# Attention weights spread over a head's dimensions through DRAM instead of through TensorE

## The reference, cut to what matters

```
q, k, v = split(layernorm(x) @ W_qkv.T + b_qkv)         # 16 heads of 8 dimensions
gains = softmax(q @ W_qscale.T + scale_gain)            # 11 scales for each head and position
for j in range(11):                                     # distance 2**j
    for tau in range(4):                                # offsets 0, d, 2d, 3d
        qk = sum(q * shift(k, d*tau), over a head's 8 dimensions)
        out += gains[j] * D4[tau] * qk * shift(v, d*tau)
out += softplus(bypass) * sum(q * k) * v
x += (out * sigmoid(gate)) @ W_out.T + b_out
```

## Time and profile before

| | |
|---|---|
| median of 3 runs | 1466.12 us (1459.56 to 1484.78) |
| the profiled execution | 1464.85 us, span 1463.1 us |
| TensorE busy | 1162.0 us (79%) |
| VectorE busy | 791.5 us (54%) |
| ScalarE busy | 651.2 us (45%) |
| GpSimd busy | 791.0 us (54%) |
| DMA queue of SyncE | 88.01 MB, 21.1% of 16 engines |

### The profile page before, as it was taken

The page is one execution under the profiler, slowest core; times in us unless marked ns, Lnnn a source line. Parts: engine busy times, 40 slices in busy tenths (PEclk is TensorE's granted clock), DMA queues, the critical chain, the costliest instruction groups (busy, mean ns, idle before and its releaser), DMA issues.

```text
span 1463.1 us, 32843 instructions
## 1 busy us (share of the span) xinstructions
PE 1162.0 (79%) x9942; PEld 876.2 (60%) x9942; DVE 791.5 (54%) x1723; ACT 651.2 (45%) x2050; POOL 791.0 (54%) x1274
## 2 busy tenths in 40 slices
PE   3878887887978898889987899866998767994481
PEld 2545554565655665666565667765877655884471
DVE  4878898889866776567787567431213201240111
ACT  2233332555445654566544444553553323562241
POOL 2655457655687648754468845875125433323604
PEclk9998987999979997799999578988985567997786
DMA  4700001222221112111123112333322323443442
GB/s 125 208 1 0 1 1 51 67 62 61 80 63 55 56 37 75 43 54 40 45 66 87 43 54 61 99 99 89 99 89 72 93 68 114 118 131 109 124 132 69
DMA packets 117639, 107.59 MB, mean 74 GB/s; under 512 B 15540, under 2 KB 88541, under 8 KB 117469
## 3 DMA queue, kind: packets, MB, share of 16 engines
q1 hardware_dynamic: 106704, 88.01, 21.1%
q0 software_dynamic: 8192, 16.79, 3.9%
q10 hardware_dynamic: 2573, 0.69, 0.2%
HBM read 76.73 MB, written 28.70 MB: 72 GB/s over the span
## 4 chain that ended last, share of the span: by engine, by line
PE 39%; POOL 18%; DVE 13%; issue 10%; another core or an unknown queue 8%; ACT 7%; ACTq 1%; DMA 1%; SPq 1%; DVEq 1%; POOLq 0%
PE bank L1160 9%; PE bank L1147 8%; POOL acc L799 8%; PE bank L1187 5%; POOL mom L764 3%; POOL sorted_x L822 3%; DVE made L1312 2%; DVE term L1341 2%; PE bank L1083 2%; PE bank L1124 2%; PE bank L1051 2%; PE bank L1030 2%; PE bank L1110 2%; PE bank L1140 1%
## 5 line engine op out<-in xcount | busy, mean ns | idle before, releaser
L799 POOL TENSOR_TENSOR acc<-acc,term 128x512 f32<-128x512 f32 x219 | 281.6, 1286 | 71.3 <-DVE term L1341 53.8
L1160 PE MATMUL bank<-w,hT 128*128 x1088 | 214.9, 321 | 22.7 <-ACT hT L985 12.8
L1341 DVE TENSOR_TENSOR term<-bank,V 128x512 f32<-128x512 f32 x251 | 167.9, 684 | 71.3 <-PE bank L1110 43.6
L1005 ACT ACTIVATE hid<-bank 128x16 f32<-128x16 f32 x512 | 93.0, 182 | 253.6 <-PE bank L1187 200.9
L985 ACT ACTIVATE hT<-bank,b1T 128x128 f32<-128x128 f32 x544 | 165.4, 371 | 81.3 <-PE bank L1147 64.8
L1187 PEld LDWEIGHTS bank<-hid,abcT 128*32 128x32 f32 x4096 | 88.3, 116 | 188.1 <-ACT hid L1005 105.5
L839 POOL DMA_INDIRECT back<-sorted_y,slot_i x128 | 125.2, 978 | 138.1 <-DMA sorted_y<-ysb 52.9
L1160 PEld LDWEIGHTS bank<-w,hT 128*128 128x128 f32 x1088 | 172.3, 219 | 40.5 <-issue 35.2
L1187 PE MATMUL bank<-hid,abcT 128*32 128x16 f32 x4096 | 138.0, 200 | 65.5 <-ACT hid L1005 57.8
L1312 DVE SCALAR_TENSOR_TENSOR made<-bank,qkvb,K 128x512 f32<-128x512 f32 x251 | 176.2, 741 | 15.7 <-PE bank L1083 6.8
L1147 PE MATMUL bank<-xTb,w1b 128*128 128x128 f32 x864 | 165.6, 320 | 7.8 <-ACT xTb L973 7.6
(11 more groups left out here) (177 smaller groups left out, 2190.6 us busy)
## 6 DMA issues: line engine op xcount, KB each, us to landing
w1b<-in_W SPq DMA_DIRECT2D x130, 256.0 KB
K<-in_W SPq DMA_DIRECT2D x54, 256.0 KB, 2.7
xsb<-sorted_x SPq DMA_DIRECT2D x184, 64.0 KB
sorted_y<-ysb SPq DMA_DIRECT2D x136, 64.0 KB
X<-in_x SPq DMA_DIRECT2D x64, 64.0 KB
out_x<-X SPq DMA_DIRECT2D x64, 64.0 KB
sorted_x<-K SPq DMA_DIRECT2D x14, 256.0 KB, 3.6
sorted_y<-made SPq DMA_DIRECT2D x48, 64.0 KB
```

The source lines that it names most:

```text
L799: nc.gpsimd.tensor_tensor(acc[:], acc[:] if k > 1 else term[0][:], term[k % NTERM][:], ALU.add).then_inc(S["terms_added"], 1)
L1005: nc.scalar.activation(hid[n % 2][:, cs], bank[6 + n % 2][:, cs], ACT.Tanh).then_inc(S["h_ready"], 1)
L1160: last = nc.tensor.matmul(bank[SLOT_BANK[place(n)]][:, 0:D], tile(hT[place(n)], c), w2[:, ds(second[n] + c * D, D)], start=(c == 0), stop= ...
L1341: V_.tensor_tensor(term[k % NTERM][:], bank[2 + k % 2][:], V[:, at:at + CW], ALU.mult).then_inc(S["terms_ready"], 1)
```

## The change

`pack` stays. Its result `wt[g]` is written to DRAM (`wstore`, at most 256 KB; two buffers for each g), and for each shift one DMA reads 16 rows back, each eight times (`fetch`, 128 rows of 2 KB, 256 KB), into a ring of seven tiles `spread` in SBUF. `high`, `low` and the spreading products on TensorE go; the product for term 0 stays and moves into bank 1. A term is now made in place in its tile, from two SBUF operands; term 0 goes straight into `acc`. Both new DMAs stand in SyncE's queue, in the planner's order, with the experts' loads and stores. A fetch waits until its tile's former term has been added, seven fetches before. reduce of the next chunk waits for this chunk's packs only; qproj of the next chunk waits for term 0; the normalised chunk `xn` gets memory of its own and no longer waits for adds.

```diff
-NPROD, NTERM = 7, 4
+NPROD, SPREAD_RING = 7, 7
...
-                free = [("low", before, 2 * g + h) for h in range(len(halves(before, g)))] if i and g < 2 else [] if g < 2 else \
-                    [("spread", before, last_term(before, 2)) if i and active(before)[2] else None]
+                free = [("wstore", before, g) if i and (g < 2 or active(before)[2]) else None]
...
             piece("PE", "reduce", i, b, [0, 0.85, 1.0, 1.15, 1.35][len(x)], USUAL,
                   [("product", i, x[-1]), ("reduce", i, b - 1) if b else None,
-                   ("term", before, last_term(before)) if i else None])
+                   past("pack", before, 0), past("pack", before, 1)])
...
+        for g in range(3 if g2 else 2):
+            piece("SP", "wstore", i, g, 0.1, USUAL,
+                  [("pack2", i, 0) if g == 2 else ("pack", i, g), ("term", i - 2, last_term(i - 2)) if i >= 2 else None], lands=2.6)
         for j, s in enumerate(sums):
...
+                piece("SP", "fetch", i, j, 0.1, USUAL,
+                      [("wstore", i, s.g), ("fetch", *fetched_for(f - 1)) if f else None,
+                       ("add", *fetched_for(f - SPREAD_RING)) if f >= SPREAD_RING else None], lands=3.2)
+            piece("DVE", "term", i, j, 0.72, USUAL,
+                  [("fetch", i, j) if j else ("spread", i, 0), ("vcopy", i, 0), ("term", i, j - 1) if j else past("out", before)])
...
+                elif what == "wstore":
+                    if k < 2:
+                        sp.wait_ge(S["packed"], nth("pack", n, k))
+                    else:
+                        sp.wait_ge(S["bank0_taken"], in_turn("reduce2", n))
+                    if n >= 2:
+                        sp.wait_ge(S["terms_ready"], nth("term", n - 2, last_term(n - 2)))
+                    h = H * len(active(n)[k]) if k < 2 else H
+                    sp.dma_start(wd[k][n % 2][0:h, :], wt[k][0:h, :]).then_inc(weights_out[k][n % 2], 16)
+                elif what == "fetch":
+                    s, f = terms(n)[k], fetch_of(n, k)
+                    sp.wait_ge(weights_out[s.g][n % 2], weights_stored(n, s.g))
+                    if f >= SPREAD_RING:
+                        sp.wait_ge(S["terms_added"], nth("add", *fetched_for(f - SPREAD_RING)))
+                    sp.dma_start(spread[f % SPREAD_RING][:],
+                                 bass.AP(wd[s.g][n % 2].tensor, s.m * H * CW, [[CW, H], [0, HD], [1, CW]])).then_inc(
+                                     spread_in[f % SPREAD_RING], 16)
...
-                    nc.gpsimd.tensor_tensor(acc[:], acc[:] if k > 1 else term[0][:], term[k % NTERM][:],
+                    nc.gpsimd.tensor_tensor(acc[:], acc[:], spread[fetch_of(n, k) % SPREAD_RING][:],
                                             ALU.add).then_inc(S["terms_added"], 1)
...
-                elif what == "high":
...
-                        pe.wait_ge(S["products_ready"], nth("product", n - 1, len(products(n - 1)) - 1))
+                        pe.wait_ge(S["terms_ready"], nth("term", n - 1, 0))
...
+                    nc.tensor.matmul(bank[1][:], blkw[:], prod[j % NPROD], start=True, stop=True).then_inc(S["spread_ready"], 1)
...
-                elif what == "low":
...
+                        if n:
+                            dve.wait_ge(S["bank0_filled"], in_turn("out", n - 1))
+                        dst, weights = acc[:], bank[1][:]
+                    else:
+                        u, turn = fetch_of(n, k) % SPREAD_RING, fetch_of(n, k) // SPREAD_RING
+                        dve.wait_ge(spread_in[u], 16 * (turn + 1))
+                        dst = weights = spread[u][:]
+                    V_.tensor_tensor(dst, weights, V[:, at:at + CW], ALU.mult).then_inc(S["terms_ready"], 1)
```

More of the change, by code:

```diff
@@ L217, in timeline @@
         piece("ACT", "vcopy", i, 0, 0.7, USUAL, [("vproj", i, 0)], bank0=0)
-        piece("PE", "qproj", i, 0, 1.1, USUAL, [("xcopy", i, 0), ("product", before, nb - 1) if i else None])
+        piece("PE", "qproj", i, 0, 1.1, USUAL, [("xcopy", i, 0), past("term", before, 0)])
         for h in range(2):
@@ L268, in timeline @@
[L268 to L274, removed]
+            if j == 0:
+                piece("PE", "spread", i, 0, 1.1, USUAL, [("product", i, n - 1)])
+            else:
+                f = fetch_of(i, j)
+                piece("SP", "fetch", i, j, 0.1, USUAL,
+                      [("wstore", i, s.g), ("fetch", *fetched_for(f - 1)) if f else None,
+                       ("add", *fetched_for(f - SPREAD_RING)) if f >= SPREAD_RING else None], lands=3.2)
@@ L452, in fillings @@
         elif what == "qproj":
-            reader[1] = "product", n, len(products(n)) - 1
+            reader[1] = "term", n, 0
         elif what == "reduce" and k == 0:
@@ L456, in fillings @@
             reader.pop(3)
-        elif what == "spread" and k >= last_term(n) - 1:
-            reader[2 + k % 2] = "term", n, k
+        elif what == "reduce" and k == len(batches(n)) - 1:
+            reader[2], reader[3] = ("pack", n, 0), ("pack", n, 1)
         end = BEGIN[key] + WORK[key][1]
@@ L574, in build @@
         th, acc = sb("th", [P, CW]), sb("acc", [P, CW])
-        term = [sb(f"term{j}", [P, CW]) for j in range(NTERM)]
-        xn = term[3]
+        xn = sb("xn", [P, CW])
         made = sb("made", [P, NPROD * CW])
@@ L583, in build @@
         wt = [sb(f"wt{g}", [P, CW]) for g in range(3)]
-        spreads = [[sb(f"spreads{g}{h}", [P, CW], F32R) for h in range(2)] for g in range(2)]
+        spread = [sb(f"spread{u}", [P, CW]) for u in range(SPREAD_RING)]
         w1b = [sb(f"w1b{u}", [P, NH]) for u in range(W_RING)]
@@ L677, in normalised, with weights_stored @@
             return xnj[p % XN_RING] if p < LATE else V[:, (p - LATE) * CW:(p - LATE + 1) * CW]
+        def weights_stored(n, g):
+            return 16 * sum(1 for c in range(n % 2, n + 1, 2) if g < 2 or active(c)[2])
         def of_part(n, k):
@@ L935, in _ @@
                     act.wait_ge(S["bank0_filled"], in_turn("rows", n, k))
[L936 to L939, removed]
+                    if n and (k < 2 or active(n - 1)[2]):
+                        act.wait_ge(weights_out[k][(n - 1) % 2], weights_stored(n - 1, k))
                     h = P if k < 2 else H
                     nc.scalar.activation(wt[k][0:h, :], bank[0][0:h, :], ACT.Copy).then_inc(S["bank0_taken"], 1)
-                elif what == "high":
[L943 to L948, removed]
                 elif what == "tanh":
@@ L1078, in _ @@
                     if k == 0 and n:
-                        pe.wait_ge(S["terms_ready"], nth("term", n - 1, last_term(n - 1)))
+                        pe.wait_ge(S["packed"], max(nth("pack", n - 1, g) for g in range(2)))
                     for j in batch:
```

72 lines of the change are left out of this document (18 added, 54 removed).

## The result

The changed kernel takes 1545.82 us (median of 4 runs, 1530.94 to 1560.11), the kernel before 1462.9 us (4 runs): a ratio of 1.049, interval 1.041 to 1.058. It is slower by 83 us on the medians. Executions of a kernel fall into a faster and a slower group, the slower at a lower granted clock; medians are of all, the ratios and intervals compare the faster ones alone, and by those the change costs 72 us (1534.0 against 1461.8). The profiled execution took 1537.06 us, of which the span is 1535.0.

The account below looks back on a forecast made before the run. It took VectorE (83% busy) to decide until 425 us, then TensorE (88%) beside VectorE (68%). Up to gate 8 +40, chunks 9 to 12 +4, chunks 13 to 15 -6, handover +10: +48 on 1464.85, 1513 us, range 1405 to 1590.

Parts of the forecast that it names:

- the port: VectorE terms with two SBUF inputs and GpSimd's adds exclude each other: 0.73 us more a term, bounds 0 and 1.00.
- the relief: Work that goes: TensorE's 235 products (127 us, partly kept), VectorE's 63 lows and 15 us of idle waits before terms.
- the DMAs: Weights stored to DRAM and fetched: 5 us more from pack to first weighted term, bounds 3 and 10, bare at chunk 12.
- the handover: At chunk 12, which closes job 3, slots wait for attention: +5 us for DMAs, +4.6 for pairs, together +10.
- rival 4: With its relief TensorE falls more often to the lower clock: 1606 us, chance 0.04.
- the sign: For rival 4, the granted clock would be below 0.85 from 425 to 704 us.
- For most chunks it is covered by the next softmax: Between chunks, the added store and fetch delay is hidden, except where a job waits for the chunk, as at chunk 12.
- My 15% more for the DMA engines: 235 fetches, 62 MB, add some 15% to the 17 to 22% DMA share in attention's stages; bandwidth isn't short.
- Rival 1: TensorE's relief wins, terms mostly miss the adds: 1382 us without port cost, about 1405 with a fifth; chance 0.22.
- Rival 2: VectorE becomes the bound, every term goes behind another and pays 1.00 us: 1592 us, chance 0.14.
- Rival 3: In SyncE's queue, fetches waiting for late adds hold slots' loads or stores: 33 us on the forecast, 1546 us; chance 0.10.
- Rival 5: Port and relief cancel within 29 us: near 1470 us, chance 0.10.

Follow-up runs that it names:

- e1: Kernel before in its own order, terms from the second on reading a constant SBUF tile instead of PSUM weights: 1457.95 us against 1377.66.
- e4: Kernel before without high, low and all spreads but the first, terms reading a constant SBUF tile, no weights stored or fetched: 1438.2 us, 1.043 of before.
- e3: Kernel before without high, low and all spreads but the first, terms reading PSUM bank 2 as it stands, 737 fillers: 1359.75 us, 0.990 of before.
- e9: Repeat of e3 (kernel before without high, low and spreads, 737 fillers) on another call: 1371.68 us, 0.982 of before.
- e2: Changed kernel with all DMAs, waits and order, but each fetched term has V as its only SBUF input: 1388.89 us, 1.010 of before.
- e8: e3 with the filler share at 0.43, 466 useless TensorE products instead of 737: 1489.34 us, 1.015 of before.
- e10: Changed kernel with fillers in 90% of a planned gap instead of 65%, 1061 instead of 749: 1453.51 us, 1.045 of before.
- e6: Changed kernel with SyncE's last setup DMAs issued behind chunk 0's fetches: 1537.08 us, 1.050 of before.
- e7: Changed kernel ordered by a planner that knows measured costs of terms, adds, SyncE's issues and landings, 892 fillers: 1528.11 us.
- e11: Kernel before with fillers in 90% of a planned gap, 694 instead of 486: 1373.05 us against 1391.71, 0.987 of before.

## Why the prediction was right, and where it was not

The direction and the mechanism held. I forecast 1513 us (+48) in 1405 to 1590; it is 1545.8 (+83). That it came so near is partly luck: the port was priced some 42 us too high, the relief 60 too high and the DMAs 24 too low, and the first of these hides part of the others. The sum's three kinds of terms, against the runs that isolate them:

| | in the sum | measured |
|---|---|---|
| the port | 87 x 0.83 = 72, 47 x 0.68 = 32, 37 x 0.34 = 13, and 4.6 at the handover: +122 us | +69 to +80 (e1), +78 (e4 less e3) |
| the relief (lows, waits, spreads) | VectorE 39 x 0.83 = 32, 11 x 0.68 = 8, 8 x 0.34 = 3; TensorE 21 + 16: 80 us less | 18 to 20 us less (e3, e9) |
| the DMAs | +5, at one handover | +29 without the port (e2 less e3) |

**The port.** The step is shown: e1 changes one operand's place and pays 69 to 80 us. Its size was too big. I took 0.73 us a term, six of 16 back to back behind adds; the terms took 0.50 us more in the changed kernel (1185 less 684) and 0.38 in e1. 97 of the 235 terms took under 0.75 us. The trace shows one reason: a term whose add hasn't begun finds the port free, and VectorE can run several terms before GpSimd gets in (at 255.62 us three terms in 1.88 us). Scaled to 0.50 my 122 us would be 83.

**The relief.** This is the term that failed most, in the direction that made my forecast too low. I priced TensorE's 127 us by its busy share, gave half back to the fillers, and counted lows and waits fully. Both repeats give 18 to 20 us at the end. Up to job 3's last slot their traces are 46 and 37 us ahead, so part was there and lost again behind attention. The engines did get their relief. VectorE's busy time over the span fell from 791.5 to 736.5 us in e3, TensorE's from 1162.0 to 1095.6 (e9: 1107.9), so giving back half to the fillers (92.1 to 122.1 us of them) was about right. What failed is the weighting: I added up both engines' savings at their busy shares as if each reached the end, and a quarter of that sum arrived. What held the end instead is shown only in part.

e8 shows why fewer fillers are no way out, a cause that I had as rival 4, with a chance of 0.04, and as an alternative to the relief: with the spreads gone TensorE idles more, its granted clock is 0.83 in place of 0.90, and what stays on it gets slower. In the changed kernel the clock from 425 to 704 us is 0.79, below the 0.85 that I had named as the sign. Rival 4's price (1606 us) was too high; its sign is there, and what the clock costs the changed kernel isn't shown, since e10's fillers raised it to 0.81 only. The Trainium skill (TensorE: Matmul & The Clock Gate, Part 1) calls half rate the idle state. Between e9 and e8 the windows agree with it: TensorE is busy 292 and 274 of the first stage's 375 us, at a clock of 0.89 and 0.83. Busy time alone doesn't order all kernels, as the changed one has 267 us at 0.87. How the loss divides between clock and time spent on fillers stays open.

**The DMAs.** "For most chunks it is covered by the next softmax" was too kind. The first chunk has no cover: VectorE stood 13.0 us for the first fetch behind SyncE's setup, which I hadn't looked at, though the burst of setup stores was in my own rows. e6 moves it and gate 0 is 11 us earlier. In all, VectorE waits 38.4 us for fetches, and 80.7 once the port is out of the way, which speaks for an overlap of the two costs; the times (e4) leave it open. My 15% more for the DMA engines was of the whole span, and it came out so (35.8% in place of 21.1); but the fetches fall into attention's stages, where the share rose by 20 to 28 points.

**The path.** I placed the handover at chunk 12 and job 3. Gate 12 came where I said (about 750, measured 753.9), gate 8 later (465, measured 486; it is 61 us late between neighbours at 37 and 49, so part of that is the new order). But the end followed job 2: 49 us late at gate 9, 65 at its last routing logits, where terms stood ahead on VectorE, and 75 after the scatters on GpSimd. I had named the reach of a delay and not these engines' queues.

**The rivals.** Rival 1, TensorE's relief with the port mostly missed, is refuted by e2 and e3: even with no port and no DMA it is 18 us, where the rival needed some 80. Rival 2 didn't come, since terms do find gaps: 0.50 us more per term, where it needed 0.9. (Its sum leaves out chunks 13 to 15, and the 4.6 us at the handover are 17 x 0.26 = 4.4; neither changes a reading.) Rival 3, SyncE's order, I can't settle: in the changed kernel TensorE waited 36.9 us for slots' positions, where it was 9.7, and SyncE 62.6 us for adds, but no run moves the fetches to another queue. e7 shows that order as a whole was worth 32 to 41 us with fillers mixed in. Rival 5 is out: the interval starts at 1.041.

## What to carry to other kernels

Before an operand of VectorE moves from PSUM to SBUF, look at what GpSimd reads at that time: one pair in the old trace gave the price of a pair here (1.69 us, where 1.75 is common in the changed kernel) but not how often it is paid, and one run with a constant operand (e1) proves it without building the change. Relief for an engine that isn't the single bound should be tested by leaving the work out (e3) before paying for its replacement; here it was 1 to 2%. A queue that gains new work has to be read from its first instruction on, the setup too.

## What the runs showed of the hardware

- VectorE, with two SBUF inputs, and GpSimd exclude each other in both directions. A term took 3.69 us at 393.78 us while GpSimd ran an add and L835 one after the other, up to 396.91. An add that started in the second of three terms took 2.46 us, the 1.1 that was left of the terms and its own 1.29:

```profile
255.62 1.88 DVE L1335 TENSOR_TENSOR spread<-spread,V 128x512 f32<-128x512 f32 x3
...
256.38 2.46 POOL L830 TENSOR_TENSOR acc<-acc,spread 128x512 f32<-128x512 f32 x1
```

  So it isn't strictly one for one, as I had assumed from a single pair: it looks as if instructions that stand ready on one engine can keep the port. The Trainium skill (SBUF — State Buffer, Who interferes with whom) speaks of the loser being blocked for the whole instruction; here it was for more than one.
- Taking work off TensorE made a kernel slower (e8, 1.015, 1.008 to 1.023), with a granted clock of 0.83 and 0.81 against 0.90 and 0.91. Adding useless work to the kernel before may have made it faster (e11, 0.987, 0.975 to 0.999).
- The same kernel took 1378, 1392 and 1462 us on three chips, 6% apart, while its repeats on one chip lie within about 2%. Ratios within a chip are what can be compared. The traces of the kernel before (slowest chip) and of e11 (1392 us chip) are level at 966.6 us and end at 1463.1 and 1385.4, with a granted clock of 0.77 and 0.86 from 935 to 1290 us. So what sets the chips apart seems to lie behind attention; e11's fillers are mixed in, and there is no trace of the kernel before on the faster chips.
